# The opening of a fused Mamba-2 mixer and MLP kernel: rows of x by batch, three first differences on VectorE, another order on ScalarE, an earlier first state sum, an identity turned on TensorE

## The reference

```python
x = x + mamba2_mixer(layernorm(x))     # W_in 512x2368, 64 heads of 16, state 128, 4 conv taps
x = x + swiglu_mlp(layernorm(x))       # 512 -> 1408 -> 512
# mixer:
z, xBC, dt = split(h @ W_in * mup)
xBC = silu(causal_conv(xBC) + conv_b);   X, B, C = split(xBC)
dt = softplus(dt + dt_bias);  dA = exp(-exp(A_log) * dt)
state = state * dA + (dt * X) B^T;       y = state C + D * X       # over time, per head
g = y * silu(z);  g = g * rsqrt(mean(g^2) + eps) * norm_w;         out = g @ W_out
```

## Time and profile before

| | |
|---|---|
| runs | 776.48, 776.4, 781.58 us; median 776.48 |
| the profiled execution | 774.75 us, its span (first to last instruction) 773.0 us |
| busy share of the span | PE 96%, PEld 79%, DVE 67%, ACT 64%, POOL 38% |
| mean granted TensorE clock | 0.985 |
| chain of waits, share of the span | PE 61%, DVE 21%, ACT 10%, issue 5%, DMA 2% |

### The profile page before, as it was taken

The page is one execution under the profiler, slowest core; times in us unless marked ns, Lnnn a source line. Parts: engine busy times, 40 slices in busy tenths (PEclk is TensorE's granted clock), DMA queues, the critical chain, the costliest instruction groups (busy, mean ns, idle before and its releaser), DMA issues.

```text
span 773.0 us, 20312 instructions
## 1 busy us (share of the span) xinstructions
PE 742.7 (96%) x8486; PEld 612.8 (79%) x8486; DVE 518.6 (67%) x845; ACT 492.7 (64%) x933; POOL 294.0 (38%) x235
## 2 busy tenths in 40 slices
PE   4887999999999999999999999889999999999998
PEld 4866888788887887887888887678888888888887
DVE  6968976886887797797797698763633532632331
ACT  6989978978978977978888888634312321321330
POOL 2173285366456536627708718540010011002002
PEclk9978999999999999999999999989999999999999
DMA  9823244484475266365376377855113003003002
GB/s 298 236 67 109 55 95 111 96 243 127 83 213 169 80 148 214 99 148 188 93 204 190 83 200 234 230 159 164 55 56 109 0 28 136 0 14 93 3 1 84
DMA packets 42300, 94.97 MB, mean 123 GB/s; under 512 B 9889, under 2 KB 15777, under 8 KB 42017
## 3 DMA queue, kind: packets, MB, share of 16 engines
q1 hardware_dynamic: 42208, 93.67, 42.6%
HBM read 84.73 MB, written 17.57 MB: 132 GB/s over the span
## 4 chain that ended last, share of the span: by engine, by line
PE 61%; DVE 21%; ACT 10%; issue 5%; DMA 2%; SPq 1%; POOL 1%; DVEq 0%; ACTq 0%; POOLq 0%
PE ps_y L1684 10%; PE ps_proj L1671 10%; DVE cx L936 9%; PE ps_out L1671 6%; PE ps_x L1671 6%; PE ps_proj L1223 4%; PE ps_proj L1224 3%; PE ps_proj L1225 3%; PE ps_x L1272 3%; PE ps_y L1295 3%; DVE ring L991 3%; ACT ring L715 2%; PE ps_out L1319 2%; DVE dt_p L911 2%; PE ps_out L1321 2%
## 5 line engine op out<-in xcount | busy, mean ns | idle before, releaser
L530 POOL TENSOR_TENSOR ring<-tokd,ring 128x1024 f32<-128x1024 f32 x64 | 122.5, 1927 | 189.4 <-ACT tokd L710 126.1
L1223 PE MATMUL ps_proj<-xn_hi,win_x_hi 128*128 128x256 f32 x352 | 104.7, 297 | 1.6 <-DVE xn_lo L905 1.6
L1224 PE MATMUL ps_proj<-xn_lo,win_x_hi 128*128 128x256 f32 x352 | 100.2, 285 | 0.0
L1225 PE MATMUL ps_proj<-xn_hi,win_x_lo 128*128 128x256 f32 x352 | 99.9, 284 | 0.0
L936 DVE SCALAR_TENSOR_TENSOR cx<-cin,consts,cx 128x256 f32<-128x256 f32 x240 | 96.4, 484 | 0.0
L1540 POOL TENSOR_TENSOR res<-res,hidden 128x512 f32<-128x512 f32 (+1 forms) x16 | 20.1, 1257 | 166.3 <-DVE hidden L1603 160.7
L1223 PEld LDWEIGHTS ps_proj<-xn_hi,win_x_hi 128*128 128x128 f32 x352 | 67.6, 192 | 14.8 <-issue 11.5
L991 DVE TENSOR_TENSOR ring<-ring,ps_tok 128x1024 f32<-128x1024 f32 x64 | 75.6, 1215 | 4.7 <-ACT ring L719 4.7
L1223 PE MATMUL ps_proj<-xn_hi,win_z_hi 128*128 128x256 f32 x256 | 74.4, 291 | 0.0
L715 ACT ACTIVATE ring<-ring 128x1024 f32<-128x1024 f32 x64 | 66.8, 1060 | 10.2 <-POOL ring L530 10.2
L1224 PE MATMUL ps_proj<-xn_lo,win_z_hi 128*128 128x256 f32 x256 | 72.5, 283 | 0.0
(11 more groups left out here) (186 smaller groups left out, 1889.6 us busy)
## 6 DMA issues: line engine op xcount, KB each, us to landing
ring<-cum_dram SPq DMA_DIRECT2D x128, 256.0 KB, 5.0
xin<-x SPq DMA_DIRECT2D x8, 512.0 KB, 3.9
res<-x SPq DMA_DIRECT2D x32, 128.0 KB, 2.7
x_dram<-res SPq DMA_DIRECT2D x32, 128.0 KB, 3.1
res<-x_dram SPq DMA_DIRECT2D x16, 256.0 KB, 2.7
out<-res SPq DMA_DIRECT2D x15, 256.0 KB, 2.1
x_in_sb<-x_dram SPq DMA_DIRECT2D x3, 1024.0 KB, 5.6
gate_w_copy<-gate_w SPq DMA_DIRECT2D x4, 704.0 KB, 5.9
```

What stands on the lines that cost most here:

```text
L530: pool.tensor_tensor(ring[:, g, :, :], own, ring[:, g, :, :], ALU.subtract).then_inc(diffed, 1)
L1223: pe.matmul(out, hi[:, k, :], xn_hi[:, k, :], start=(k == 0), stop=False)
L1224: pe.matmul(out, hi[:, k, :], xn_lo[:, k, :], start=False, stop=False)
L1225: made = pe.matmul(out, lo[:, k, :], xn_hi[:, k, :], start=False, stop=(k == KT - 1))
```

## The change

Five edits, all in the opening and in the first block:

1. x's first block is loaded as two transfers, one for each batch, the first with a semaphore of its own. Statistics, scale and normalisation of the opening go batch by batch; `weight_lo(0)` goes behind both normalisations, `weight_hi(1)` and `weight_lo(1)` behind `norm_hi` and `norm_lo`. The masks on GpSimd wait for the normalisation.
2. Of the first step's four differences, VectorE makes three (`opening_diff`, around `weight_lo(8)`), GpSimd the fourth, behind them.
3. ScalarE keeps `tok` first and alternates clamp and fade; `weight_hi(9)` moves from ahead of the body to behind the second fade, and `weight_lo(9)` on VectorE behind the second mix.
4. `update_state(0, 0)` moves ahead of the statistics of block 1; the first state copy waits until ten low halves are made (their raw values lie in `state` and its neighbours).
5. TensorE turns the identity 20 times ahead of the first `turn_xn` and 6 times behind the second, into a bank that nothing reads.

```diff
--- before.py
+++ after.py
@@ -219,6 +219,7 @@
         hi_made, lo_made = sem("hi_made"), sem("lo_made")
         zeroed, filled = sem("zeroed"), sem("filled")
         a_made, a_negated = sem("a_made"), sem("a_negated")
+        x_first = sem("x_first")
         x_in, xres_in = sem("x_in"), [sem(f"xres_in{j}") for j in range(STEPS)]
         ring_in = [sem(f"ring_in{n}") for n in range(RING)]
         cum_out, whole_out, whole_in = sem("cum_out"), sem("whole_out"), sem("whole_in")
@@ -313,7 +314,8 @@
 
         @block.sync
         def _(sp):
-            sp.dma_start(xin[:], x_by_block[0]).then_inc(x_in, 16)
+            sp.dma_start(xin[:, 0, :], x_by_block[0, :, 0, :]).then_inc(x_first, 16)
+            sp.dma_start(xin[:, 1, :], x_by_block[0, :, 1, :]).then_inc(x_in, 16)
             sp.dma_start(consts[:], packed).then_inc(consts_in, 16)
             for n in range(PIECES):
                 raw = piece(n)[2]
@@ -505,12 +507,19 @@
             def norm_scale(j):
                 pool.wait_ge(moments_made, 2 * j + 2)
                 pool.tensor_tensor(spread[:], moments[:, :, 1], eps[:], ALU.add).then_inc(eps_added, 1)
-                pool.wait_ge(eps_added, j + 1)
+                pool.wait_ge(eps_added, j + 2)
                 pool.tensor_tensor(rstd[:], spread[:], minus_half[:], ALU.pow).then_inc(rstd_made, 1)
 
-            norm_scale(0)
+            def opening_scale(b):
+                pool.wait_ge(moments_made, b + 1)
+                pool.tensor_tensor(spread[:, b:b + 1], moments[:, b, 1:2], eps[:, b:b + 1], ALU.add).then_inc(eps_added, 1)
+                pool.wait_ge(eps_added, b + 1)
+                pool.tensor_tensor(rstd[:, b:b + 1], spread[:, b:b + 1], minus_half[:, b:b + 1], ALU.pow).then_inc(rstd_made, 1)
+
+            opening_scale(0)
+            opening_scale(1)
             pool.memset(chain[:, 0::Q], 0.0).then_inc(filled, 1)
-            pool.wait_ge(rstd_made, 1)
+            pool.wait_ge(xn_made, 2)
             for b in range(BATCH):
                 pool.wait_ge(filled, b + 2)
                 pool.affine_select(out=causal[half(b), :], in_=causal[half(b), :], compare_op=ALU.is_ge, fill=0.0, base=0,
@@ -600,9 +609,8 @@
                         rms_scale(c - 1, 1 - j)
 
             pool.wait_ge(filled, 4)
-            pool.wait_ge(tap_made, N_TAPS)
-            for g in range(GROUPS):
-                diff(0, 0, g)
+            pool.wait_ge(diffed, GROUPS - 1)
+            diff(0, 0, GROUPS - 1)
             body(0, True, False)
             for i in range(1, BLOCKS - 1):
                 body(i, False, False)
@@ -753,17 +761,27 @@
                 c = STEPS * i
                 if not first:
                     evacuate(i, 6)
-                clamp(c, 0)
-                clamp(c, 1)
-                if not first:
+                if first:
+                    keep_tok(c)
+                    clamp(c, 0)
+                    fade(c, 0)
+                    clamp(c, 1)
+                else:
+                    clamp(c, 0)
+                    clamp(c, 1)
                     square(c - 1)
                     evacuate(i, 7)
-                keep_tok(c)
-                fade(c, 0)
-                clamp(c, 2)
+                    keep_tok(c)
+                    fade(c, 0)
+                    clamp(c, 2)
                 fade(c, 1)
+                if first:
+                    weight_hi(9)
+                    clamp(c, 2)
+                    fade(c, 2)
                 clamp(c, 3)
-                fade(c, 2)
+                if not first:
+                    fade(c, 2)
                 fade(c, 3)
                 if first:
                     weight_hi(EVENTS)
@@ -831,10 +849,9 @@
                 gate_hi(c)
 
             weight_hi(0)
-            weight_hi(1)
             norm_hi(0, 0)
             norm_hi(0, 1)
-            for n in range(2, 6):
+            for n in range(1, 6):
                 weight_hi(n)
             act.wait_ge(zeroed, 7)
             evacuate(0, 0)
@@ -858,7 +875,6 @@
             conv_silu(0, CONV_ORDER[6:10])
             keep_halo(0)
             evacuate(0, 7)
-            weight_hi(9)
             body(0, True, False)
             for i in range(1, BLOCKS - 1):
                 body(i, False, False)
@@ -893,8 +909,26 @@
                 for b in range(BATCH):
                     dve.bn_aggr(moments[:, b, :], stats[:, b, :]).then_inc(moments_made, 1)
 
+            def opening_stats(b):
+                dve.wait_ge(x_in if b else x_first, 16)
+                dve.bn_stats(stats[:, b, :], xin[:, b, :]).then_inc(stats_made, 1)
+                dve.wait_ge(stats_made, b + 1)
+                dve.bn_aggr(moments[:, b, :], stats[:, b, :]).then_inc(moments_made, 1)
+
+            def opening_normalise(b):
+                dve.wait_ge(rstd_made, b + 1)
+                dve.tensor_scalar(xin[:, b, :], xin[:, b, :], moments[:, b, 0:1], rstd[:, b:b + 1],
+                                  ALU.subtract, ALU.mult).then_inc(xn_made, 1)
+
+            def opening_diff(g):
+
+                dve.wait_ge(ring_in[g], 32)
+                dve.wait_ge(tokd_kept, 1)
+                own = tokd[:, 0, CUM, g * GH:(g + 1) * GH].unsqueeze(2).to_broadcast([P, GH, Q])
+                dve.tensor_tensor(ring[:, g, :, :], own, ring[:, g, :, :], ALU.subtract).then_inc(diffed, 1)
+
             def normalise(j):
-                dve.wait_ge(rstd_made, j + 1)
+                dve.wait_ge(rstd_made, j + 2)
                 for b in range(BATCH):
                     dve.tensor_scalar(xin[:, b, :], xin[:, b, :], moments[:, b, 0:1], rstd[:, b:b + 1],
                                       ALU.subtract, ALU.mult).then_inc(xn_made, 1)
@@ -995,6 +1029,7 @@
                 dve.wait_ge(update_made, 2 * c + h + 1)
                 s, new = state[:, :, h * 512:(h + 1) * 512], ps_x[:].rearrange("p (b n) -> p b n", b=BATCH)
                 if c == 0:
+                    dve.wait_ge(lo_made, EVENTS)
                     dve.tensor_copy(s, new).then_inc(state_made, 1)
                     return
                 dve.wait_ge(state_faded, c)
@@ -1036,15 +1071,18 @@
                     low_max(i - 1, 1)
                 mask_cb(c)
                 make_xpad(i, 0)
-                if first:
-                    weight_lo(9)
-                else:
+                if not first:
                     make_x1(c - 2)
                 mix(c, 0)
                 if not first:
                     scale_carry(i, 0)
-                for g in range(1, GROUPS):
-                    mix(c, g)
+                mix(c, 1)
+                if first:
+                    weight_lo(9)
+                mix(c, 2)
+                mix(c, 3)
+                if first:
+                    update_state(c, 0)
                 if not last:
                     norm_stats(i + 1)
                     normalise(i + 1)
@@ -1052,7 +1090,8 @@
                     weight_lo(EVENTS)
                 if last:
                     mlp_stats(0)
-                update_state(c, 0)
+                if not first:
+                    update_state(c, 0)
                 if last:
                     mlp_normalise(0)
                     mlp_normalise(1)
@@ -1165,13 +1204,14 @@
                                   hand.xn_hi[:, :, t * P:(t + 1) * P], ALU.subtract).then_inc(hand.split, 1)
 
             mlp.vector_ahead(dve)
-            norm_stats(0)
+            opening_stats(0)
+            opening_stats(1)
+            opening_normalise(0)
+            opening_normalise(1)
             weight_lo(0)
-            normalise(0)
-            weight_lo(1)
             norm_lo(0, 0)
             norm_lo(0, 1)
-            for n in range(2, 6):
+            for n in range(1, 6):
                 weight_lo(n)
             for n in range(1, LOGN):
                 soft(0, n)
@@ -1187,7 +1227,10 @@
             weight_lo(7)
             conv_taps(0, CONV_ORDER[6:8])
             conv_taps(0, CONV_ORDER[8:10])
+            opening_diff(0)
             weight_lo(8)
+            opening_diff(1)
+            opening_diff(2)
             dve.wait_ge(zeroed, 8)
             body(0, True, False)
             for i in range(1, BLOCKS - 1):
@@ -1201,6 +1244,12 @@
 
         @block.tensor
         def _(pe):
+            def keep_warm(n):
+
+
+                for _ in range(n):
+                    pe.transpose(ps_out[:, 0:P], eye[:], eye[:])
+
             def turn_xn(j, b, opening=False):
                 pe.wait_ge(xn_made, 2 * j + b + 1)
                 if not opening:
@@ -1416,8 +1465,10 @@
                     project(i + 1, 7)
 
             pe.wait_ge(filled, 1)
+            keep_warm(20)
             turn_xn(0, 0, True)
             turn_xn(0, 1, True)
+            keep_warm(6)
             for e in range(8):
                 pe.wait_ge(lo_made, e + 1)
                 project(0, e)
```

## The result

| | before | after |
|---|---|---|
| median | 776.4 us (7 runs) | 787.38 us (7 runs) |
| profiled execution | 774.75 us, span 773.0 | 790.63 us, span 788.9 |
| mean granted TensorE clock | 0.985 | 0.982 |

The ratio is 1.0134 with a 95% interval of 1.0099 to 1.0168: the change costs 11 us, 1.3%. The forecast was 776.7 us and its range ended at 779.5.

What follows compares the result with a forecast made beforehand. TensorE's stream, busy 96% of the span, was taken as the bound. 773.0 + 0.5 (opening) + 0 + 0 - 0.3 (state's sum) = 773.2 us of span, hence median 776.7; range 773.9 to 779.5.

Steps and rivals of the forecast that it cites:

- the first paragraph's conclusion: Whole kernel: TensorE is busy 96%, so opening and first-block edits move only what its stream waits for at the start.
- the turns of the identity at nothing: Opening, TensorE: 20 turns take 4.9 us, ending at 7.0, hold the real turn by 0.3 at most; 6 fit a wait.
- no case reaches that: Whole kernel: 1% is about 7.8 us; the largest win was put at 2.8, the largest loss at 3.7.
- the 0.02 for slower: Whole kernel: chance of a measured slowdown beyond 1%, kept for what was not seen; within 1% had 0.96.
- The opening: First projection at 9.6 instead of 11.73, event 1 over at 13.9, then TensorE idles 3.0 us until the first evacuation.
- the term for the clock: Event 2 after the idle: low clock puts ScalarE's third evacuation at 21.3, a loss of 0.5; bounds -0.95 and +1.25.
- The extra load's issue: SyncE's queue in the opening: one more issue of 0.44 us ahead of later weights, taken as 0; bounds 0 and +0.44.
- The differences at 0: First step: three differences go to VectorE and hide behind ScalarE, price 0, both bounds 0.
- ScalarE's order: First block, 39.6 to 49.7: same steps reordered; the last mix follows its fade at once, VectorE through at 50.9: 0.3 won.
- The state's sum: First block's end: moved ahead of the next block's statistics, 0.7 possible, 0.3 taken as gain; bounds -0.7 and +2.0.
- the collision that it named: First block's end: GpSimd's third difference of the next step falls on VectorE's low halves, costing up to 2.0.
- Rival (b): First block: GpSimd difference collides with VectorE's low weights, +2.0, and event 2 is low throughout, +1.25: 779.7; 17%.

Runs made afterwards that it cites:

- after shifted back: The changed kernel with 14 turns of the identity instead of 20 and 54 small matmuls more, a shift of 255 places: 780.19 us, ratio 1.0054.
- the kernel before with the two late loads moved: The kernel before with the last two MLP up-weight loads (704 KB each) placed behind the last x rows: 776.95 us, ratio 1.0017.

## Why the prediction was wrong

The sign and the size were missed, and one step did it.

- **The step that failed** is the first paragraph's conclusion: that an edit of the opening "can win or lose only what that stream waits for at the start", and with it, in the sum, the turns of the identity at nothing. I costed the 26 turns as work, 4.9 us beside a wait, and not as 52 places in an instruction stream that arrives in blocks of 256. The missing term is 7 to 10 us: 8.0 by 51 empty instructions, 10.0 by the same in the changed kernel without turns, 7.2 by after against after shifted back. From it follows "no case reaches that" for 1%, and the 0.02 for slower: I had taken chances over cases of one region only. The page's row of 67 instruction packets, and before's own 1.95 at 509.80 with the releaser "issue", were there to be read.
- **The opening was right in its mechanism.** First projection 9.34 (forecast 9.6), event 1 over at 14.06 (13.9), weight 5 at 14.57 (14.07 to 14.5), idle 3.47 (3.0), then the low clock. The size was off: the term for the clock was 0.5 with a bound of 1.25, and ScalarE was 1.17 late, of which 0.58 is event 2's later start, behind the later weight 5. One pair of executions is a weak measure of this, though: the kernel before with the two late loads moved has the same opening and passes the third evacuation at 22.00 and not at 20.81, because its pace doubles at 17.8 and not at 15.6. What holds over the traces is the order of the groups: the changed openings without turns pass it at 20.2 to 21.5, the two with turns at 21.98 and 22.43. The gain of 2.4 us at the projection (2.1 forecast) does not get past the first evacuation. The kernel before with the turns (idle 0.81, clock at 1.00) shows the same rule from the other side. The Trainium skill's rule, page "TensorE: Matmul & The Clock Gate" (HAM oscillation), by which a burst behind a wait starts cold, agrees with 0.72 here and with 0.50 behind the stall at 226.
- **The extra load's issue** was taken at 0 with a bound of 0.44. Weight 5 came 0.50 later. No run undoes the split load alone, and the scatter is larger: its start lies between 13.68 and 15.46 in the kernels with one load, between 14.09 and 15.08 in those with two. Whether the issue costs anything is not shown.
- **The differences at 0** were right: three on VectorE took 1.23 and 2.36 for two, and ScalarE had no gap over 0.1 in that stretch.
- **ScalarE's order** was said to win 0.3 and loses about 0.25. Clamp and fade of one group now follow each other, and each fade waits for its own clamp: in the kernel without turns a clamp that starts at 43.18 has its fade at 44.26, 1.08 later, where before's two fades in a row stand 0.95 apart (1.99 for two). I had added durations and forgotten the hand-over within one engine.
- **The state's sum** was to win 0.3 (0.7 less a collision). From the third evacuation to the next block's first it is 47.2 us against 45.9: 1.2 lost, inside the bound of 2.0. Two things stand behind it, and they do not simply add. The sum itself stands ahead of statistics that ScalarE waits for, which the prediction put at nothing and the traces, without a collision, at 0.9 to 1.4. And the collision that it named does come, on the second pair of low halves (3.05 against 1.40) as forecast; the normalise collides as well (4.16 for two; before, only one of them took 2.13), but that happens without the early sum too.
- **Rival (b)**, block and low clock together at 779.7, is the nearest to what is left when the placement is taken away, 780.2. That is partly luck: in that kernel the second pair of low halves does not collide at all (1.40), so (b)'s term of 2.0 is not what fills the sum.

## What to carry to other kernels

Before pricing instructions added to the busiest engine, read the instruction queue's packets and every "issue" gap of its timeline: added instructions shift all later block boundaries, and a boundary under full transfer engines can cost several microseconds and the clock behind it. The boundaries can be counted off a trace: here TensorE's instruction 193 + 256 k. To judge an edit by what it does, compare it at equal placement: pad the stream to a whole block (here to within one instruction), or add as many empty instructions to the kernel before. And a warm-up is worth something only if the next wait goes too: in the changed kernel it made the wait longer.

## What the runs showed of the hardware

- TensorE's instructions come in packets of 16 KB (1.10 MB in 67), 256 instructions each, through the same engines as the data. A packet takes 0.9 to 1.6 us (27 of the 1,141 in the 17 traces took up to 3.2). A TensorE that waited for one goes on 1.2 to 1.7 us after its end. One that met eight loads of 256 KB started 5.3 us later than with these cut to a sixteenth.
- No packet starts more than 300 instructions ahead of its boundary, in 17 traces.
- The stall of after is twofold: 3.65 us of standing, then a granted clock of 0.50 for at least 6 us. Behind both the delay is 6.5 us larger.
- 51 empty semaphore increments cost 8.0 us; 64 small matmuls near the same place (ratio 1.0013) cost nothing that can be told from no change.
- A stall of this kind is not made good later: from step 6 to step 14 of after the delay stays within 10.6 to 11.5 us.
